# One transformer layer on eight cores: layer-norm output and softmax sums moved from GpSimd to VectorE, value projection done once per stage

## The chip, the cores and the metric

The kernel runs on all 8 cores of one Trainium2 chip. Every core does the same program on its own 4096 of the 32768 tokens, and no core waits for another. The metric is the device time of the slowest core in microseconds (us).

## The reference

The layer attends over the 16 heads of one token, not over tokens, so every token is independent of the others.

```python
q = x @ Wq + bq
kv = (x @ Wdown + bdown) @ Wup + bup
q = q.reshape(B, T, H, Dh)
k, v = jnp.split(kv.reshape(B, T, H, 2 * Dh), 2, axis=-1)
q = apply_rope(q)
k = apply_rope(k)
att = jnp.einsum('bthd,btgd->bthg', q, k) / jnp.sqrt(jnp.float32(Dh))
att = jax.nn.softmax(att, axis=-1)
out = jnp.einsum('bthg,btgd->bthd', att, v)
x = _layernorm(x + out.reshape(B, T, D) @ Wout + bout)
h = jax.nn.silu(x @ wg.T / 127) * (x @ wu.T / 127)
x = _layernorm(x + h @ wdn.T / 127)
```

D is 1024, H is 16, Dh is 64, the latent width is 256 and the hidden width 3072. The rotation of q and k depends on the token alone, and both q and k of a product belong to the same token, so it drops out of att and the kernel leaves it away.

## The kernel before

All activations lie transposed: 128 features in the partitions, tokens along the columns. After a part that turns the weights to bf16 and stores them again in DRAM (the first 350 us), a core works through 8 stages of 512 tokens (`ST`). A stage has a main chain of work, planned into one list per engine:

- `plan_head`: x is loaded by DMAs of the POOL queue (L294), the latent is computed (L313, evacuated by L323), then q with weight tiles `wqb`, eight DMAs of the SP queue into two buffers (matmuls L346, evacuation L357).
- For each half of 256 tokens (`HF`): `plan_kv_part` computes k for all 16 heads (matmuls L588, ScalarE evacuation L603 into `krep`) and then v in the same way into `vdup0` or `vdup1`. `plan_sc` multiplies q by each head's k on VectorE (L622 into `hadb`, two buffers), sums over features on TensorE (L647) and takes the exponential on ScalarE (L634 into `e_sb`).
- `plan_av`: GpSimd adds the 16 exponentials (L668 and fourteen times L674 into `esum32`), VectorE takes the reciprocal (L677), casts it (L679) and scales `e_sb` by it in eight operations (L685). Then, 64 times, TensorE spreads weights to 128 partitions (L738, `selz_sb`), VectorE multiplies them by v (L701 into `p_sb`, two buffers), and TensorE adds up the product (L754, `id_sb`); ScalarE evacuates the sum (L706, `avn`).
- `plan_wo`: output projection with weight tiles `wob` (L792), and the residual on VectorE (L805). The projection of the first half is planned after the scores of the second.
- The first layer norm ends with sixteen VectorE operations of 512 columns, eight times a multiplication (L895) and an addition (L899), which write the input of the feed-forward part.

Beside it, in stage s, runs a second chain, `plan_ffn_ch2`, the feed-forward part of stage s-1: 24 tiles m, each with a gate (L397, eight matmuls) and an up product (L407, eight), `silu` on ScalarE (L416) and a product on VectorE (L423, `h_sb`), then 192 matmuls of the down projection (L450) with their residual (L459). The two weight tiles of an m, `wgb` and `wub`, are DMAs of the POOL queue. Both buffers are double, the second DMA waits until the first has landed since they count on one semaphore, and the gate product waits for both. The second layer norm ends with the scale and shift of the output: for each of 8 pieces GpSimd multiplies (L522 into `lnscr2`) and adds (L530 into `x2b`, two buffers), and a DMA of the SP queue stores the piece to `yt`. The addition of piece J waits until the store of piece J-2 has landed.

The order of the two chains on each engine is set by a list scheduler at build time. It knows a cost `d` of every operation and emits, at each step, the operation that can start first:

```python
key = (round(es / 800.0), -CP[id(nd)], es)
if best is None or key < best[0]:
    best = (key, k, ch, nd, es)
```

Within a chain nothing overtakes on its engine, and at run time each engine goes through its list in order. Changed costs or queues therefore change how the chains are interleaved on all five queues. All DMAs of the second chain and of q and the output projection are written by one helper, L263.

## Time and profile before

| what | value |
|---|---|
| runs shown | 3774.47 and 3853.24 us, median 3813.85 us |
| profiled execution | 3772.72 us, its span 3771.2 us on the slowest core |
| spans of the eight cores | 3746.8 to 3771.2 us |
| mean granted TensorE clock of the slowest core | 0.893 |
| PE busy | 2767.9 us, 73% |
| DVE (VectorE) busy | 1565.3 us, 42% |
| ACT (ScalarE) busy | 823.7 us, 22% |
| POOL (GpSimd) busy | 625.7 us, 17% |

Busy time is the share of the span in which an engine executes; a matmul's busy time holds its latency too, so it overlaps with the next one's. A view of waits names, for each idle gap of an engine, the instruction that ended it. The program starts with 346 us in which TensorE has nothing to do, the stages begin then; stage 0 has no feed-forward part beside it, and after the last stage one feed-forward part runs alone.

### The profile page before, as it was taken

How to read it: one execution, taken by the hardware profiler on the slowest of the kernel's cores; microseconds unless marked ns; L12 is line 12 of the kernel's file. 1: busy time of each engine (PE TensorE's matmuls, PEld its weight loads, DVE VectorE, ACT ScalarE, POOL GpSimd, SP SyncE). 2: the span in 40 equal slices, each digit the busy share in tenths (PEclk: the TensorE clock that was granted, in tenths of full speed). 3: DMA queues.
4: the chain of work that ended last, by engine and by line, in shares of the span. 5: the costliest groups of instructions: out<-in, count | busy, mean ns of one | idle time of the engine just before them, and what ended most of it. 6: DMA issues, size and time to landing. Idle time of an engine off the chain costs nothing.

```text
span 3771.2 us, 42195 instructions; the slowest of 8 cores (3746.8 to 3771.2 us)
## 1 busy us (share of the span) xinstructions
PE 2767.9 (73%) x12672; PEld 1093.4 (29%) x12672; DVE 1565.3 (42%) x2086; ACT 823.7 (22%) x1479; POOL 625.7 (17%) x908
## 2 busy tenths in 40 slices
PE   0002686789877988698968996798779896989565
PEld 0000221333323333233322432333333332333122
DVE  2221444354444444453545353544444445535210
ACT  0000220314023312322140404140233223221100
POOL 0111101011121120312021112111211203110312
PEclk9999665889988999899988999899889998999688
DMA  6886001112231232223221323123312312221222
GB/s 192 241 241 178 9 1 34 51 36 73 78 108 30 65 84 67 73 59 87 71 75 52 92 65 95 40 70 82 94 41 62 89 58 87 62 79 59 95 78 73
DMA packets 108706, 303.98 MB, mean 81 GB/s; under 512 B 16192, under 2 KB 24768, under 8 KB 108496
## 3 DMA queue, kind: packets, MB, share of 16 engines
q1 hardware_dynamic: 61520, 169.14, 15.3%
q0 software_dynamic: 46976, 132.15, 12.2%
q8 instruction: 118, 1.93, 0.2%
q14 instruction: 92, 0.75, 0.1%
HBM read 269.77 MB, written 39.85 MB: 82 GB/s over the span
## 4 chain that ended last, share of the span: by engine, by line
PE 56%; DMA 9%; POOL 8%; issue 7%; DVE 6%; ACT 4%; POOLq 0%; DVEq 0%; ACTq 0%; SPq 0%
PE P L450 10%; PE P L738 9%; PE P L397 8%; PE P L407 8%; PE P L754 7%; PE P L647 6%; POOL esum L674 4%; DMA wgb<-wg_s 3%; DMA wub<-wu_s 3%; PE P L588 3%; DVE p_sb L701 3%; POOL lnscr L522 2%; POOL x2b L530 2%; PE P L792 2%; DVE hadb L622 1%
## 5 line engine op out<-in xcount | busy, mean ns | idle before, releaser
L701 DVE TENSOR_TENSOR p_sb<-P,vdup 128x512 bf16<-128x512 f32 x1024 | 697.7, 690 | 503.9 <-PE P L754 385.5
L397 PE MATMUL P<-x_bf,wgb 128*128 128x512 bf16 x1536 | 535.0, 414 | 163.2 <-DMA wub<-wu_s 163.1
L738 PE MATMUL P<-e_sb,selz_sb 16*128 16x512 bf16 x1024 | 431.5, 430 | 137.7 <-DVE e_sb L685 92.9
L754 PE MATMUL P<-p_sb,id_sb 128*128 128x256 bf16 x2048 | 501.8, 303 | 37.8 <-DVE p_sb L701 33.1
L450 PE MATMUL P<-h_sb,wdb 128*128 128x512 bf16 x1536 | 509.0, 397 | 13.7 <-DVE r_bf L459 13.1
L407 PE MATMUL P<-x_bf,wub 128*128 128x512 bf16 x1536 | 518.8, 399 | 0.0
L622 DVE TENSOR_TENSOR hadb<-q_sb,krep 128x2048 bf16<-128x2048 bf16 x256 | 309.3, 1224 | 431.0 <-PE P L647 292.0
L647 PE MATMUL P<-hadb,selred_sb 128*16 128x256 bf16 x2048 | 325.3, 276 | 45.2 <-DVE hadb L622 19.9
L423 DVE TENSOR_TENSOR h_sb<-s_sil,P 128x512 bf16<-128x512 bf16 x192 | 131.3, 684 | 413.6 <-PE P L407 298.9
L313 PE MATMUL P<-x_bf,wd_sb 128*128 128x512 bf16 x128 | 36.0, 431 | 352.5 <-DMA x_bf<-xt 352.5
L706 ACT ACTIVATE avn<-P 128x256 bf16<-128x256 f32 x128 | 49.2, 384 | 989.7 <-PE P L754 975.6
L397 PEld LDWEIGHTS P<-x_bf,wgb 128*128 128x128 bf16 x1536 | 150.4, 102 | 380.4 <-issue 299.9
L792 PE MATMUL P<-avn,wob 128*128 128x256 bf16 x1024 | 236.5, 283 | 31.0 <-DMA wob<-wout_s 19.4
L263 POOL DMA_DIRECT2D wgb<-wg_s x192 | 105.8, 551 | 896.7 <-PE P L407 818.1
L416 ACT ACTIVATE s_sil<-P 128x512 bf16<-128x512 f32 x192 | 114.4, 596 | 626.1 <-PE P L397 625.6
L754 PEld LDWEIGHTS P<-p_sb,id_sb 128*128 128x128 bf16 x2048 | 180.3, 101 | 229.2 <-issue 187.4
L738 PEld LDWEIGHTS P<-e_sb,selz_sb 16*128 16x128 bf16 x1024 | 91.4, 93 | 485.2 <-issue 485.2
L522 POOL TENSOR_TENSOR lnscr<-r_bf,rstd 128x512 f32<-128x512 bf16 x64 | 84.5, 1321 | 870.1 <-DVE nmb L513 862.1
L647 PEld LDWEIGHTS P<-hadb,selred_sb 128*16 128x16 bf16 x2048 | 153.2, 89 | 216.9 <-issue 193.6
L407 PEld LDWEIGHTS P<-x_bf,wub 128*128 128x128 bf16 x1536 | 153.0, 101 | 209.4 <-issue 112.9
L346 PE MATMUL P<-x_bf,wqb 128*128 128x512 bf16 x512 | 134.4, 415 | 105.8 <-DMA wqb<-wq_s 90.0
L450 PEld LDWEIGHTS P<-h_sb,wdb 128*128 128x128 bf16 x1536 | 146.1, 99 | 218.8 <-issue 124.3
(69 smaller groups left out, 2141.3 us busy)
## 6 DMA issues: line engine op xcount, KB each, us to landing
wdb<-wdn_s SPq DMA_DIRECT2D x64, 768.0 KB, 4.3
wgb<-wg_s POOLq DMA_DIRECT2D x192, 256.0 KB, 3.0
wub<-wu_s POOLq DMA_DIRECT2D x192, 256.0 KB, 2.9
wob<-wout_s SPq DMA_DIRECT2D x128, 256.0 KB, 2.8
wqb<-wq_s SPq DMA_DIRECT2D x64, 256.0 KB, 3.1
yt<-x2b SPq DMA_DIRECT2D x64, 256.0 KB, 2.1
stg<-wg SPq DMA_DIRECT2D x24, 512.0 KB, 5.0
stg<-wu SPq DMA_DIRECT2D x24, 512.0 KB, 5.3
```

The source lines that it names most:

```text
L346: e.matmul(o, l, r, start=st, stop=sp)),
L397: e.matmul(o, l, r, start=st, stop=sp)),
L407: e.matmul(o, l, r, start=st, stop=sp)),
L450: e.matmul(o, l, r, start=st, stop=sp)),
L522: b=rstd2[:, :]: e.tensor_mul(o, a, b)),
L622: add('V', (lambda e, o=o, a=q3, b=b: e.tensor_mul(o, a, b)), waits=tuple(w), inc=s_v, d=1460)
L647: e.matmul(o, l, r, start=st, stop=sp)),
L674: e.tensor_tensor(o, a, b, ALU.add)),
L701: add('V', (lambda e, o=o, a=a, b=b: e.tensor_mul(o, a, b)), waits=w, inc=s_v, d=640)
L738: e.matmul(o, l, r, start=True, stop=True)),
L754: e.matmul(o, id_sb[:, :], r, start=st, stop=sp)),
L792: e.matmul(o, l, r, start=st, stop=sp)),
```

## The change

Three edits. The sixteen operations that scale and shift the output of the second layer norm go from GpSimd to VectorE. The fifteen additions of exponentials go from GpSimd to VectorE, in the main chain. And v is computed once per stage for all 512 tokens into `vdup_all`, by sixteen pairs of 512-column matmuls and sixteen 512-column evacuations, in place of two times sixteen of 256 columns; the multiplication L701 then reads two pieces of 256 columns that lie 512 apart. GpSimd keeps only its DMAs, and its two semaphores are dropped. Line numbers after the change move by some 2 to 24.

```diff
-        vdup = [E(nc.sbuf_tensor(f"vdup{i}", [128, NH * HF], BF16)) for i in range(2)]
+        vdup_all = E(nc.sbuf_tensor("vdup_all", [128, NH * ST], BF16))
...
             for J in range(XC):
-                w = [(s_v2, ck['nmb2_v']), (s_v2, r2_v[J]), (s_gv2, s_gv2.c)]
-                add('G', (lambda e, o=lnscr2[:, :], a=r2_bf[:, J * ST:(J + 1) * ST],
+                add('V', (lambda e, o=lnscr2[:, :], a=r2_bf[:, J * ST:(J + 1) * ST],
                           b=rstd2[:, :]: e.tensor_mul(o, a, b)),
-                    waits=w, inc=s_gv2, d=1000)
-                w = [(s_gv2, s_gv2.c)]
+                    waits=[(s_v2, s_v2.c)], inc=s_v2, d=830)
+                w = [(s_v2, s_v2.c)]
                 val = outb[J % 2] + 16 * (J // 2) if J >= 2 else outb[J % 2]
                 if val > 0:
                     w.append((s_out[J % 2], val))
                 o = x2b[J % 2][:, :]
-                x2_v.append(add('G', (lambda e, o=o, a=lnscr2[:, :], b=nmb2[:, :]:
+                x2_v.append(add('V', (lambda e, o=o, a=lnscr2[:, :], b=nmb2[:, :]:
                                       e.tensor_add(o, a, b)),
-                                waits=w, inc=s_gv2, d=1000))
+                                waits=w, inc=s_v2, d=830))
...
+            def plan_vd():
+                pe0, sc0 = s_pe.c, s_s.c
+                for g in range(NH):
...
+                    for c in range(2):
+                        o = P[5 + g % 2][:, 0:ST]
+                        l = wupv_sb[:, g * 256 + c * 128:g * 256 + (c + 1) * 128]
+                        r = lat_bf[:, c * ST:(c + 1) * ST]
+                        add('T', (lambda e, o=o, l=l, r=r, st=(c == 0), sp=(c == 1):
+                                  e.matmul(o, l, r, start=st, stop=sp)),
...
+                    o = vdup_all[:, g * ST:(g + 1) * ST]
+                    i_ = P[5 + g % 2][:, 0:ST]
+                    b = bupv_sb[:, g:g + 1]
+                    evs.append(add('S', (lambda e, o=o, i=i_, b=b:
+                                         e.activation(o, i, AF.Identity, bias=b)),
+                                   waits=tuple(w), inc=s_s, d=770))
...
                 for g in range(2, NH):
                     a2 = e_sb[:, g * HF:(g + 1) * HF]
-                    add('G', (lambda e, o=esum32[:, :], a=esum32[:, :], b=a2:
+                    add('V', (lambda e, o=esum32[:, :], a=esum32[:, :], b=a2:
                               e.tensor_tensor(o, a, b, ALU.add)),
-                        waits=[(s_s, exp_g(g)), (s_gv, s_gv.c)], inc=s_gv, d=450)
+                        waits=[(s_s, exp_g(g)), (s_v, s_v.c)], inc=s_v, d=420)
...
-                        b = vdup[hf][:, gp * 512:(gp + 1) * 512]
+                        b = vdup_all[0:128, 0:NH * ST].rearrange(
+                            "p (g t) -> p g t", g=NH)[:, 2 * gp:2 * gp + 2,
+                                                      hf * HF:hf * HF + HF]
...
             kd0 = plan_kv_part(0, 0)
-            vd0 = plan_kv_part(0, 1)
+            vd_all = plan_vd()
             exp_end0, had0 = plan_sc(0, kd0)
-            avn_end0, erep_end0 = plan_av(0, exp_end0, vd0)
+            avn_end0, erep_end0 = plan_av(0, exp_end0, vd_all)
             kd1 = plan_kv_part(1, 0, guard=[(s_v, ck['avtt_end'][0])])
-            vd1 = plan_kv_part(1, 1)
```

The scheduler's new order shows in three places.

First, SyncE's queue (SP) at a boundary of two stages. Before, with `wqb` the weight tiles of q for the next stage, `yt` the stores of the finished output and `wdb` tiles of the down projection:

```order
L263 DMA wqb<-wq_s 128x1024 x2
L263 DMA yt<-x2b 128x512 x3
L263 DMA wqb<-wq_s 128x1024
L263 DMA yt<-x2b 128x512
L263 DMA wqb<-wq_s 128x1024
L263 DMA yt<-x2b 128x512
L263 DMA wqb<-wq_s 128x1024
L263 DMA yt<-x2b 128x512
L263 DMA wqb<-wq_s 128x1024
L263 DMA yt<-x2b 128x512 x2
L263 DMA wdb<-wdn_s 128x3072 x2
L263 DMA wqb<-wq_s 128x1024 x2
```

and now:

```order
L261 DMA wqb<-wq_s 128x1024 x2
L261 DMA yt<-x2b 128x512 x2
L261 DMA wqb<-wq_s 128x1024 x6
L261 DMA yt<-x2b 128x512
L261 DMA wob<-wout_s 128x1024
L261 DMA yt<-x2b 128x512
L261 DMA wob<-wout_s 128x1024
L261 DMA yt<-x2b 128x512 x4
L261 DMA wdb<-wdn_s 128x3072 x2
```

The stores of the output stood between the tiles of q; now all tiles of q but the first two stand together, and six stores and the two down tiles stand behind them. In the other boundaries seven tiles stand ahead of the first store.

Second, GpSimd's queue (POOL) from the same boundary into the next stage. Before:

```order
L522 TENSOR_TENSOR lnscr<-r_bf,rstd 128x512
L530 TENSOR_TENSOR x2b<-lnscr,nmb 128x512
L263 DMA wgb<-wg_s 128x1024
L263 DMA wub<-wu_s 128x1024
L263 DMA wgb<-wg_s 128x1024
L263 DMA wub<-wu_s 128x1024
L668 TENSOR_TENSOR esum<-e_sb 16x256
L674 TENSOR_TENSOR esum<-esum,e_sb 16x256 x14
L263 DMA wgb<-wg_s 128x1024
L263 DMA wub<-wu_s 128x1024
```

and now:

```order
L292 DMA x_bf<-xt 128x512 x8
L261 DMA wgb<-wg_s 128x1024
L261 DMA wub<-wu_s 128x1024
L261 DMA wgb<-wg_s 128x1024
L261 DMA wub<-wu_s 128x1024
L261 DMA wgb<-wg_s 128x1024
L261 DMA wub<-wu_s 128x1024
```

The weights of the first two tiles stood behind the output of the layer norm, and those of the third behind the additions of exponentials; both are gone from the queue.

Third, TensorE at the end of the scores of a first half (`hadb`) and the begin of the weighted sum (`selz_sb`). Before:

```order
L647 MATMUL P<-hadb,selred_sb 16x256 x24
L407 MATMUL P<-x_bf,wub 128x512
L397 MATMUL P<-x_bf,wgb 128x512 x8
L407 MATMUL P<-x_bf,wub 128x512 x8
L738 MATMUL P<-e_sb,selz_sb 128x512 x2
L397 MATMUL P<-x_bf,wgb 128x512 x4
L738 MATMUL P<-e_sb,selz_sb 128x512
```

and now, from the last of the scores on (ahead of it stand the up product of m=0, the 16 matmuls of m=1, and the last two groups of scores with five gate matmuls of m=2 between them):

```order
L671 MATMUL P<-hadb,selred_sb 16x256
L395 MATMUL P<-x_bf,wgb 128x512 x3
L405 MATMUL P<-x_bf,wub 128x512 x8
L395 MATMUL P<-x_bf,wgb 128x512 x8
L762 MATMUL P<-e_sb,selz_sb 128x512 x2
L405 MATMUL P<-x_bf,wub 128x512 x8
L762 MATMUL P<-e_sb,selz_sb 128x512
```

Some 24 more matmuls of the feed-forward part (m=2 whole, the gate of m=3) now stand ahead of the weighted sum. Of the second half's k part, where 56 feed-forward matmuls stood between 64 of k and v, 30 now stand between 32 of k.

## Rows read from the trace of the kernel before

**Rows 1.** Windows (us; busy PE, PEld, DVE, ACT, POOL; clock; DMA; GB/s): a stage, a part
```profile
1901.00:2298.60 397.60, 331.00 (x1586) 134.06 (x1584) 187.05 (x248) 105.40 (x188) 68.28 (x100) 0.94 0.24 71
...
2074.70:2096.10 21.40, 20.40 (x121) 10.54 (x120) 4.45 (x6) 16.74 (x37) 3.42 (x7) 1.00 0.26 76
```

**Rows 2.** Waits of PE over the whole span: us in total, times, longest
```profile
PE P L397 <- DMA wub<-wu_s: 163.1, 58, 26.8
PE P L738 <- DVE e_sb L685: 92.9, 10, 15.6
PE P L346 <- DMA wqb<-wq_s: 90.0, 33, 13.5
```

**Rows 3.** Timeline of a boundary: start, us, engine, operation [idle before it <-what ended it]
```profile
1903.04 1.57 DVE L895 TENSOR_TENSOR lnscr<-r_bf,rstd 128x512 f32<-128x512 bf16 x1
...
1904.20 1.43 POOL L522 TENSOR_TENSOR lnscr<-r_bf,rstd 128x512 f32<-128x512 bf16 x1
...
1920.18 0.61 POOL L263 DMA_DIRECT2D wgb<-wg_s  x1
...
1920.80 0.82 SPq L263 DMA_DIRECT2D wdb<-wdn_s  x2
...
1927.90 0.55 POOL L263 DMA_DIRECT2D wub<-wu_s  x1 [7.11 <-DMA wgb<-wg_s]
...
1932.62 5.16 PE L346 MATMUL P<-x_bf,wqb 128*128 128x512 bf16 x16 [13.48 <-DMA wqb<-wq_s]
```

**Rows 4.** Timeline of PE in the q part after stage 0
```profile
710.42 3.61 PE L346 MATMUL P<-x_bf,wqb 128*128 128x512 bf16 x16 [0.93 <-ACT lat_bf L323]
...
725.02 3.80 PE L346 MATMUL P<-x_bf,wqb 128*128 128x512 bf16 x16 [0.77 <-DMA wqb<-wq_s]
```

**Rows 5.** ACT: evacuations of v in one half (timeline), of k and q (groups, mean ns)
```profile
1947.39 8.68 ACT L603 ACTIVATE vdup<-P,bupv_sb 128x256 bf16<-128x256 f32 x16
...
L603 ACT ACTIVATE krep<-P,bupk_sb 128x256 bf16<-128x256 f32 x256 | 118.5, 474 | 56.5 <-PE P L588 55.0 <-issue 0.3
...
L357 ACT ACTIVATE q_sb<-P,bq_sb 128x512 bf16<-128x512 f32 x64 | 44.0, 687 | 194.0 <-PE P L346 194.0
```

**Rows 6.** Timeline from the additions of exponentials to the first weighted sums
```profile
1977.67 11.09 POOL L674 TENSOR_TENSOR esum<-esum,e_sb 16x256 f32<-16x256 f32 x14
...
1988.93 1.74 DVE L677 RECIPROCAL zinv<-esum 16x256 f32<-16x256 f32 x1 [6.10 <-POOL esum L674]
...
1990.77 0.28 DVE L679 CAST zinvb<-zinv 16x256 bf16<-16x256 f32 x1
...
1991.72 1.10 PE L738 MATMUL P<-e_sb,selz_sb 16*128 16x512 bf16 x2 [10.00 <-DVE e_sb L685]
...
1995.31 1.87 PE L397 MATMUL P<-x_bf,wgb 128*128 128x512 bf16 x4 [2.49 <-DMA wub<-wu_s]
```

**Rows 7.** VectorE's prices: groups by line, mean ns after the busy time
```profile
L701 DVE TENSOR_TENSOR p_sb<-P,vdup 128x512 bf16<-128x512 f32 x1024 | 697.7, 690 | 503.9 <-PE P L754 385.5 <-PE P L738 116.1 <-issue 0.3
...
L622 DVE TENSOR_TENSOR hadb<-q_sb,krep 128x2048 bf16<-128x2048 bf16 x256 | 309.3, 1224 | 431.0 <-PE P L647 292.0 <-PE P L588 76.1 <-ACT krep L603 57.6
...
L501 DVE TENSOR_TENSOR vpe<-vpe,musq 128x512 f32<-128x512 f32 x8 | 5.5, 692 | 29.1 <-ACT musq L498 29.1
```

**Rows 8.** Timeline: two weight DMAs of POOL in the first half's output projection
```profile
2150.98 0.55 POOL L263 DMA_DIRECT2D wgb<-wg_s  x1 [2.18 <-PE P L407]
...
2157.44 0.55 POOL L263 DMA_DIRECT2D wgb<-wg_s  x1 [1.99 <-PE P L407]
```

**Rows 9.** Timeline of DVE before the last feed-forward part, of POOL at the end
```profile
3521.22 0.69 DVE L899 TENSOR_TENSOR x_bf<-lnscr,nmb 128x512 bf16<-128x512 f32 x1
3530.73 0.69 DVE L423 TENSOR_TENSOR h_sb<-s_sil,P 128x512 bf16<-128x512 bf16 x1 [8.82 <-PE P L407]
...
3740.23 1.15 POOL L522 TENSOR_TENSOR lnscr<-r_bf,rstd 128x512 f32<-128x512 bf16 x1 [70.82 <-DVE nmb L513]
...
3760.95 1.26 POOL L530 TENSOR_TENSOR x2b<-lnscr,nmb 128x512 f32<-128x512 f32 x1 [0.20 <-POOL lnscr L522]
```

More of the change, by code:

```diff
@@ L574, in plan_kv_part @@
                 pe0, sc0 = s_pe.c, s_s.c
-                wgt = wupk_sb if part == 0 else wupv_sb
+                wgt = wupk_sb
                 for g in range(NH):
@@ L591, in plan_kv_part @@
                 for g in range(NH):
-                    dst = krep if part == 0 else vdup[hf]
-                    bias = bupk_sb if part == 0 else bupv_sb
+                    dst = krep
+                    bias = bupk_sb
                     w = list(wS([(s_pe, pe0 + g + 1)]))
                     if g == 0:
-                        if part == 0 and prev_red_end:
+                        if prev_red_end:
                             w.append((s_pe, prev_red_end))
-                        if part == 1 and ck['avtt_end'][hf]:
-                            w.append((s_v, ck['avtt_end'][hf]))
                     o, i_ = dst[:, g * HF:(g + 1) * HF], P[5 + g % 2][:, 0:HF]
@@ L604, in plan_kv_part @@
                                    waits=tuple(w), inc=s_s, d=560))
+                return evs
+            def plan_vd():
+                pe0, sc0 = s_pe.c, s_s.c
+                for g in range(NH):
+                    w = []
+                    if sc0 + g - 1 > 0:
+                        w.append((s_s, sc0 + g - 1))
+                    for c in range(2):
[4 more added lines that the diff above has]
+                                  e.matmul(o, l, r, start=st, stop=sp)),
+                            waits=(w if c == 0 else ()),
+                            inc=(s_pe if c == 1 else None), d=258)
+                evs = []
+                for g in range(NH):
+                    w = list(wS([(s_pe, pe0 + g + 1)]))
+                    if g == 0:
+                        for h2 in range(2):
+                            if ck['avtt_end'][h2]:
+                                w.append((s_v, ck['avtt_end'][h2]))
+                    o = vdup_all[:, g * ST:(g + 1) * ST]
[4 more added lines that the diff above has]
+                                   waits=tuple(w), inc=s_s, d=770))
                 return evs
@@ L666, in plan_av @@
                 exp_g = lambda g: exp_end - NH + g + 1
[L667 removed]
+                add('V', (lambda e, o=esum32[:, :], a=e_sb[:, 0:HF],
                           b=e_sb[:, HF:2 * HF]: e.tensor_tensor(o, a, b, ALU.add)),
[L669 to L670 removed]
+                    waits=wV([(s_s, exp_g(1)), (s_v, s_v.c)]), inc=s_v, d=420)
                 for g in range(2, NH):
                     a2 = e_sb[:, g * HF:(g + 1) * HF]
[L673 removed]
+                    add('V', (lambda e, o=esum32[:, :], a=esum32[:, :], b=a2:
                               e.tensor_tensor(o, a, b, ALU.add)),
[L675 to L676 removed]
+                        waits=[(s_s, exp_g(g)), (s_v, s_v.c)], inc=s_v, d=420)
                 add('V', (lambda e, o=zinv[:, :], i=esum32[:, :]: e.reciprocal(o, i)),
[L678 removed]
+                    waits=[(s_v, s_v.c)], inc=s_v, d=2100)
                 add('V', (lambda e, o=zinvb[:, :], i=zinv[:, :]: e.tensor_copy(o, i)),
```

23 lines of the change are left out of this document (8 added, 15 removed).

## The prediction, made before the changed kernel ran

> **What bounds the kernel now.** I read the page first, then the busy time of one stage, the waits of PE, and last the timeline of that stage queue by queue. A stage takes 397.6 us, of which PE is busy 331 us and DVE 187 us [rows 1]. PE does everything else waits for, so what counts is where PE stands still. Leaving the start aside, its three largest waits are 163.1 us for the weights of the feed-forward part, 92.9 us for the normalized exponentials and 90.0 us for the weights of q [rows 2]. All three lead to GpSimd. At a boundary of two stages GpSimd scales the output with operations of 1.43 us; each store to `yt` waits for one, and SyncE's queue holds the weights of q between and behind these stores, so that the last two q tiles come after 13.48 us of standing still [rows 3]. The next feed-forward weights are issued behind the same GpSimd work, at 1920.18, and the first of them needs until 1927.90 [rows 3]. Inside the stage GpSimd adds exponentials for 12 us while PE waits 10.0 us, and the weights of the third tile stand behind these additions, for another 2.49 us [rows 6]. Nothing of this is GpSimd being busy, which it is for 68 of 397.6 us; it is GpSimd's queue.
>
> **The q part (-72 us).** After stage 0 there is no second layer norm, hence no store and no GpSimd work. There the q part shows what the q tiles cost by themselves: 16 matmuls in 3.6 us, then gaps of about 0.8 us, three in all [rows 4]. Eight q parts with 2.3 us of such gaps are 18 us; the rest of the 90.0 us [rows 2], 72 us, comes from the stores, and the new order has at least six of the eight tiles in a row. What takes its place: DVE does both layer norms alone. Now they run side by side and hinder each other, 1.57 us for an operation that takes 0.69 us alone [rows 3, 9]. Sixteen of DVE's operations beside GpSimd's take about 1.6 us each with the gap, 26 us; on DVE alone 32 operations of 0.69 us and 0.1 us between them are 25 us. So the pair of norms is done as early as before, the output simply comes last. An addition that waits for a store holds up what is queued behind it on DVE, the multiplications of q by k (L622). The first two of those are ready when the q part ends, and PE needs them only after k and v, over 20 us later (8.7 us for each, [rows 5]). I count nothing for it.
>
> **v at once (+24 us), and its second half gone (-71 us).** An evacuation of 256 columns takes 0.474 us and comes every 0.54 us (8.68 by 16), because PE and ACT take turns on two banks. With 512 columns ACT needs 0.687 us, 0.21 more, and PE 0.22 more (3.61 us for 16 matmuls of 512 columns, so two times 256 columns more) [rows 4, 5]. Two banks share this, so one comes every 0.54 + 0.21 = 0.75 us: 12.1 us in place of 8.7 us in the first half, +3.4 us in 7 stages. In the second half PE's list had 56 feed-forward matmuls of 512 columns and 64 of 256 columns in the k and v part of 21.4 us [rows 1]; it now has 30 and 32. By columns that is 52%, 11.2 us, so 10.2 us less in 7 stages. The weights say the same: a tile pair comes every 6.46 us there [rows 8], and 26 matmuls are 1.6 pairs, 10.5 us. Those 26 are done earlier, in the 10 us in which PE stood still.
>
> **Sums of exponentials, first half (-29 us).** DVE's price for 16x256 float32 additions stands in no row. From below it is the cast of the same size, 0.28 us, from above GpSimd's own 0.79 us (11.09 by 14) [rows 6]. Between them I take 0.42 us: a 512-column addition takes 0.692 us and L622, which does its 2048 columns at two per step, 1.224 us for 1024 steps [rows 7], so a step costs 1.04 ns and an operation 0.16 us beside them. With 0.10 us between two operations (1988.93 + 1.74 to 1990.77) 15 of them take 7.8 us against 12.0 us: 4.2 us. The Trainium skill, page "VectorE: DVE Perf Modes", section on the TRN2 errata, gives (N+151)/0.96 ns for a float32 addition of two tensors of N columns, which it calls exact at 512, 691 ns; the trace agrees at 512 (692 ns). No run here shows 256 columns; by the page it would be 424 ns. Off the 4.2 us go two products of the feed-forward part (L423, 0.69 us) that now stand between on DVE, 1.4 us, and eight up matmuls ahead of the third broadcast on PE, some 1.1 us of which nothing hides. To it come the 2.49 us of waiting for weights [rows 6]. That makes 4.2 us in 7 stages. The new order asks for four weight tiles in a row between the up product of m=0 and the first weighted sum: at 3.2 us each (half of 6.46, [rows 8]) they have landed some 11 us after it and the gate of m=3 is done at 13.7 us; DVE's chain, counted from the same point (1.0 us for a group of scores, 1.2 us for the last multiplication, additions, reciprocal 1.74 us, cast, first scaling), ends at about 14 us. So DVE still is the last, by little.
>
> **Second half and the rest (-14, -14, -19 us).** In the second half the additions are on the path too, 4.2 us less 1.4 us of products between them; PE's list holds feed-forward work up to there, so I take 2 us in 7 stages. Stage 0 has no feed-forward part: twice 4.2 us, and v falls from 17.4 to 12.1 us, 13.7 us together. At the end, the last feed-forward part starts with weights already loaded: its first product came at 3530.73, 8.8 us after the layer norm had ended [rows 9]. With both norms on DVE the input is ready some 6 us earlier too, at about 3516, and one gate and up product at half clock takes about 4 us more; I take 10 us. The last output is 22 us of GpSimd work (3740.23 to 3762.21) [rows 9], on DVE 12.8 us, stretched to 13.5 us by the landing of stores: -8.5 us.
>
> Sum: -72 +24 -71 -29 -14 -14 -19 = -195 us. From the profiled execution's 3773 us this gives 3578 us, 5.2% less. The profiled execution lies with the lower of the two runs shown (3774); the median, 3814, holds one of 3853, and such a run of the changed kernel would be at 3650.
>
> **Rivals.** *The weights take the place of the additions.* The four tiles ahead of the weighted sum may come slowly: next to stores and `wdb` one took 7.7 us (1920.18 to 1927.90, [rows 3]) in place of 3.2. Four of them cost 18 us; less 3 us of slack and again in 7 stages that is +105 us: 3683 us. For it speaks that stores now trail into the next stage; against it that the scores come 40 us after the boundary, and that tiles in the middle of a stage come every 3.2 us [rows 8].
>
> *The moved work is worth nothing.* DVE becomes the late one: stores that wait in SyncE's queue hold its additions, q by k comes late, and the 72 us are lost; an addition costs GpSimd's 0.79 us, and 16 times 4.2 us are lost. 3578 + 72 + 67 = 3717 us, 1.5% under before. Against it: DVE is busy 187 of 397.6 us [rows 1] and gets 8 us a half and 13 us a boundary. The Trainium skill, page "Perfetto Trace Analysis", section on optimizing Scalar and DVE operations, says work may go to GpSimd when DVE is saturated, and that a move between the two might not help since they share a read port. The trace shows the sharing, 1.57 against 0.69 us, and by it the pair of norms alone gives nothing; what I expect comes from the two queues behind it.
>
> *Slower: v read with a stride.* L701 runs 1024 times, on the path, and now reads two pieces. At 0.69 us [rows 7] with 0.53 us of it for the 512 columns (1.04 ns each), half speed would give 3578 + 543 = 4121 us. It decides from 0.19 us each, and 0.27 us each are 2% slower. Against it: L622 reads q in eight pieces and k repeated, and does 2048 columns in 1224 ns [rows 7], twice the rate of L501.
>
> **How the numbers follow.** The forecast 0.65, the weights 0.17, worth nothing 0.10, the stride 0.04, something unnamed 0.04. By its own unknowns the forecast reaches down to 3500 us: additions at 0.38 us a piece are 34 us less, v hidden 24 us less, the boundaries a little shorter than counted, 20 us. Upwards, additions at 0.79 us add 67 us, and most of the rival on weights lies under 3680 us. Hence 3500 to 3680 us. Faster by over 2%, which is about what a measurement of this kernel can tell, holds the forecast, the weights and a little of the rest: 0.85; within 2% 0.10, slower 0.05.
>
> **What would show it.** Right: PE's wait for `wqb` falls from 90 to about 20 us; the additions on DVE at 0.42 us, reciprocals 8 us after the last multiplication by k; evacuations of v every 0.75 us; the k part of the second half near 11 us; L701 still at 690 ns; a stage some 23 us shorter. Wrong: waits for `wub` ahead of L738 in each stage, a wait of `x2b` for a store that reaches PE, or L701 above 0.7 us.

## The result, and the profile after

The changed kernel takes 3525.72 us (median of 11 runs, 3509.68 to 3711.7) beside 3773.32 us of the kernel before (10 runs); the ratio is 0.934, 95% interval 0.9311 to 0.9369, so 6.6% faster. The profiled execution took 3518.16 us, its span 3516.3 us, against 3771.2 us before. The forecast was 3578 us, range 3500 to 3680. Ratios below are always to the kernel before, with their 95% interval. Where half of the chip ran at a lower clock in a profiled execution (runs 5 and 8), its numbers here are those of a core of the other half.

Lines move by 2 to 24: L344 is the q part, L395 and L405 gate and up product, L585 k, L613 and L627 v, L646 the multiplication of q by k, L671 the scores, L692 and L697 the additions, L725, L762 and L778 the weighted sums, L816 the projection, L918 and L922 the first layer norm, L519 and L527 the output.

First the windows of a whole stage and of the k part of a second half, which answer to [rows 1]:

```profile
core 7: us, PE busy (x) PEld busy (x) DVE busy (x) ACT busy (x) POOL busy (x), PEclk, DMA share, GB/s
1790.50:2155.60 365.10, 326.22 (x1553) 130.79 (x1552) 197.52 (x291) 102.49 (x171) 30.55 (x56) 0.97 0.26 78
1947.90:1959.30 11.40, 10.81 (x64) 5.36 (x62) 3.28 (x4) 8.29 (x19) 1.78 (x4) 1.00 0.26 74
```

The stage is 32.5 us shorter while PE's busy time fell only from 331 to 326 us: the gain is time in which PE stood still. VectorE took over all the arithmetic of GpSimd and is busy only 10 us more. The column behind POOL says that the granted clock rose too, from 0.94 to 0.97. The waits of PE over the whole span answer to [rows 2]:

```profile
PE P L395 <- DMA wub<-wu_s: 93.0, 52, 6.6
PE P L344 <- DMA wqb<-wq_s: 40.0, 30, 2.9
PE P L762 <- DVE e_sb L707: 20.6, 2, 11.2
PE P L395 <- DVE x2b L527: 19.3, 1, 19.3
```

The three waits of [rows 2] came to 346 us and are 154 us now. The fourth line has a new name only: at the same place, ahead of the first gate product of the last feed-forward part, PE stood still before as well, and longer, and the view put it down to the weights, which were loaded behind GpSimd's output work. It is the longest wait in the first line of [rows 2]:

```profile
3524.31 3.57 PE L397 MATMUL P<-x_bf,wgb 128*128 128x512 bf16 x8 [26.80 <-DMA wub<-wu_s]
```

So of the 70 us by which the wait for `wub` fell, 26.8 us changed their name, and 19.3 us of them are still there. The boundary of two stages, as [rows 3] showed it (DVE, PE and SyncE's queue):

```profile
1795.58 0.69 DVE L918 TENSOR_TENSOR lnscr<-r_bf,rstd 128x512 f32<-128x512 bf16 x1
...
1797.87 12.13 SPq L261 DMA_DIRECT2D wqb<-wq_s  x6
1810.15 0.34 SPq L261 DMA_DIRECT2D yt<-x2b  x1
...
1811.52 3.65 PE L344 MATMUL P<-x_bf,wqb 128*128 128x512 bf16 x16 [1.93 <-DMA wqb<-wq_s]
```

Six q tiles are issued in a row and PE's gaps between them are at most 1.93 us, where one was 13.48 us. The groups by line answer to [rows 5] and [rows 7], the timeline behind the scores to [rows 6]:

```profile
L725 DVE TENSOR_TENSOR p_sb<-P,vdup_all 128x512 bf16<-128x512 f32 x1024 | 697.5, 689 | 448.2 <-PE P L778 312.5 <-PE P L762 133.5
...
L697 DVE TENSOR_TENSOR esum<-esum,e_sb 16x256 f32<-16x256 f32 x224 | 92.3, 412 | 25.2 <-ACT e_sb L658 3.6 <-DVE esum L697 0.5
...
L918 DVE TENSOR_TENSOR lnscr<-r_bf,rstd 128x512 f32<-128x512 bf16 x64 | 44.2, 691 | 6.2
...
L527 DVE TENSOR_TENSOR x2b<-lnscr,nmb 128x512 f32<-128x512 f32 x64 | 44.2, 691 | 30.1 <-DMA yt<-x2b 22.8 <-DVE lnscr L519 7.1
```
```profile
1824.88 12.05 ACT L627 ACTIVATE vdup_all<-P,bupv_sb 128x512 bf16<-128x512 f32 x16
...
1858.89 6.10 DVE L697 TENSOR_TENSOR esum<-esum,e_sb 16x256 f32<-16x256 f32 x12
...
1865.69 0.47 ACT L658 ACTIVATE e_sb<-P,cvec_sb 16x256 bf16<-16x256 f32 x1 [2.38 <-PE P L671]
...
1866.33 0.41 DVE L697 TENSOR_TENSOR esum<-esum,e_sb 16x256 f32<-16x256 f32 x1 [0.40 <-ACT e_sb L658]
```

An addition costs 412 ns (0.42 us forecast), L725 with its stride 689 ns (690 before), a layer-norm operation 691 ns (1309 beside GpSimd), an evacuation of v comes every 0.75 us (12.05 by 16, as forecast). The last three lines show something the forecast did not have: twelve additions are done before the last exponential exists; the chain of additions waits for it, not the other way round. The last exponential is late because the added feed-forward matmuls stand among the last scores.

The timelines of PE show where the time went. Each line is the length of one part of PE's list, from its first matmul to its last or to the next part, in us and summed over the seven stages 1 to 7; the last three lines are single stretches:

| part of PE's list | before | after | change |
|---|---|---|---|
| q parts | 209.7 | 145.3 | -64.4 |
| k of the first half | 84.9 | 66.3 | -18.6 |
| v of the first half | 60.8 | 85.7 | +24.9 |
| first score to first weighted sum | 251.2 | 233.4 | -17.8 |
| weighted sums, first half | 582.5 | 541.9 | -40.6 |
| k (and v) of the second half | 152.0 | 78.7 | -73.3 |
| projection to second weighted sum | 297.9 | 283.8 | -14.1 |
| weighted sums, second half | 581.9 | 550.3 | -31.6 |
| second projection | 159.7 | 170.4 | +10.7 |
| stage 0 | 358.5 | 341.1 | -17.4 |
| after the last projection | 282.8 | 273.8 | -9.0 |
| start of stage 0 | 346 | 344 | -2 |

With the small parts left out (-2) this is the 255 us between the spans. Two changes stand out, for the forecast had no term for them: the weighted sums of both halves, 72 us, whose own matmuls are as before, and the k part of the first half.

### The profile page after: what moved, and what is told of

Same layout as the page of the kernel before. It is cut to its first block, busy times and chain, and to the rows that moved or that the text cites. A ratio compares the mean times of both kernels' runs of the same rounds, so it can differ in the third digit from the quotient of the medians.

```text
span 3516.3 us, 41208 instructions; the slowest of 8 cores (3489.0 to 3516.3 us)
## 1 busy us (share of the span) xinstructions
PE 2687.4 (76%) x12416; PEld 1059.3 (30%) x12416; DVE 1668.7 (47%) x2454; ACT 807.4 (23%) x1363; POOL 292.2 (8%) x540
## 3 DMA queue, kind: packets, MB, share of 16 engines
q1 hardware_dynamic: 61520, 169.14, 16.5%
## 4 chain that ended last, share of the span: by engine, by line
PE 60%; DMA 11%; DVE 8%; issue 6%; ACT 5%; DVEq 0%; ACTq 0%; POOLq 0%; POOL 0%; SPq 0%
PE P L448 10%; PE P L762 9%; PE P L395 9%; PE P L405 8%; PE P L778 8%; PE P L671 6%; DMA wgb<-wg_s 3%; DMA wub<-wu_s 3%; DVE p_sb L725 3%; PE P L816 2%; PE P L344 2%; DMA wqb<-wq_s 2%; PE P L585 2%; PE P L613 2%; DMA wob<-wout_s 1%
## 5 line engine op out<-in xcount | busy, mean ns | idle before, releaser
L725 DVE TENSOR_TENSOR p_sb<-P,vdup_all 128x512 bf16<-128x512 f32 x1024 | 697.5, 689 | 448.2 <-PE P L778 312.5
L395 PE MATMUL P<-x_bf,wgb 128*128 128x512 bf16 x1536 | 524.2, 402 | 113.6 <-DMA wub<-wu_s 93.0
L405 PE MATMUL P<-x_bf,wub 128*128 128x512 bf16 x1536 | 494.0, 395 | 22.8 <-DVE h_sb L421 22.8
L778 PE MATMUL P<-p_sb,id_sb 128*128 128x256 bf16 x2048 | 487.0, 292 | 26.7 <-DVE p_sb L725 19.9
L448 PE MATMUL P<-h_sb,wdb 128*128 128x512 bf16 x1536 | 495.1, 387 | 13.3 <-DVE r_bf L457 12.3
L646 DVE TENSOR_TENSOR hadb<-q_sb,krep 128x2048 bf16<-128x2048 bf16 x256 | 309.6, 1223 | 349.2 <-PE P L671 261.8
L762 PE MATMUL P<-e_sb,selz_sb 16*128 16x512 bf16 x1024 | 414.3, 413 | 65.5 <-DVE p_sb L725 43.2
L671 PE MATMUL P<-hadb,selred_sb 128*16 128x256 bf16 x2048 | 327.6, 275 | 44.3 <-DVE hadb L646 19.0
L816 PE MATMUL P<-avn,wob 128*128 128x256 bf16 x1024 | 243.4, 285 | 40.0 <-DMA wob<-wout_s 28.8
L395 PEld LDWEIGHTS P<-x_bf,wgb 128*128 128x128 bf16 x1536 | 149.0, 100 | 340.3 <-issue 242.7
L778 PEld LDWEIGHTS P<-p_sb,id_sb 128*128 128x128 bf16 x2048 | 176.2, 99 | 210.1 <-issue 163.1
L671 PEld LDWEIGHTS P<-hadb,selred_sb 128*16 128x16 bf16 x2048 | 152.2, 88 | 219.5 <-issue 198.0
L405 PEld LDWEIGHTS P<-x_bf,wub 128*128 128x128 bf16 x1536 | 150.0, 100 | 225.1 <-issue 122.8
L762 PEld LDWEIGHTS P<-e_sb,selz_sb 16*128 16x128 bf16 x1024 | 90.6, 92 | 392.5 <-issue 392.5
L829 DVE SCALAR_TENSOR_TENSOR r_bf<-P,bout_sb,x_bf 128x256 bf16<-128x256 f32 x128 | 61.7, 482 | 258.2 <-PE P L816 258.2
L658 ACT ACTIVATE e_sb<-P,cvec_sb 16x256 bf16<-16x256 f32 x256 | 117.5, 465 | 228.6 <-PE P L671 228.0
```

What stands on the lines that cost most here:

```text
L395: e.matmul(o, l, r, start=st, stop=sp)),
L405: e.matmul(o, l, r, start=st, stop=sp)),
L448: e.matmul(o, l, r, start=st, stop=sp)),
L646: add('V', (lambda e, o=o, a=q3, b=b: e.tensor_mul(o, a, b)), waits=tuple(w), inc=s_v, d=1460)
L658: e.activation(o, i, AF.Exp, bias=b, scale=0.125)),
L671: e.matmul(o, l, r, start=st, stop=sp)),
```

## The experiments

Theory Q: the first edit acts through the two queues in which GpSimd's operations and the stores stood. Theory C: the weighted sums are shorter because PE no longer stands still ahead of them, and with that no longer falls to half clock (1.2 in place of 2.4 GHz, a granted clock of 0.50). The rivals: E (the first edit makes VectorE faster), O (the weighted sums are shorter through another order of the matmuls), and in the expectations of runs 6 and 7 O' (the half clock in them comes from the boundary of the stages).

**1. First edit undone.** The sixteen operations of L519 and L527 go back to `'G'` with a semaphore of their own, as in the removed lines of the diff.

> The changed kernel with the sixteen output operations of the second layer norm back on GpSimd, all else as changed. Theory Q (what the move brought is order in two queues): the stores stand between the q tiles on SyncE again, the q parts go from 126 back to about 185 us in seven stages, PE's wait for wqb from 40 to about 100 us, the first k part waits again for feed-forward weights in some stages (+20 us), the last output takes 9 us longer: about 3526 + 92 = 3618 us. Rival E (what it brought is a faster VectorE, or the q part was shortened by the other two edits): the q parts stay under 145 us, and the time rises by no more than 30 us, to 3556 us or less.

Ratio to before 0.958 (0.9523 to 0.9637), in the profile's run 3617 us. The q parts are at 204.1 us in seven stages (145.3 with the edit; the table below has all such sums), the first k parts at 86.2 (66.3), and what follows the last projection takes 288.3 us (273.8):

```profile
PE P L396 <- DMA wub<-wu_s: 134.1, 51, 27.5
PE P L345 <- DMA wqb<-wq_s: 87.6, 34, 11.1
```

As Q said. Rival E is out by the time; the next run tests it again with both engines loaded as here.

**2. The same, but GpSimd issues the stores.**

```diff
-            for J in range(XC):
                 w = [(s_gv2, x2_v[J])]
...
-                dma('Y', s_out[J % 2], dst, src, w)
+                dma('G', s_out[J % 2], dst, src, w)
```

> As the first run, but GpSimd issues the stores of the output itself, so SyncE's queue holds the eight q tiles in a row while GpSimd and VectorE still work side by side. Theory Q: the q parts stay at 120 to 135 us, so about 60 us less than the first run, 3558 us, unless the weights of the feed-forward part, now behind operations and stores on GpSimd, take it back in part. Rival E (sharing between the two engines is what costs): no better than the first run, q parts near 185 us, 3618 us.

The q parts are 152.4 us and PE waits as little for `wqb` as in the changed kernel, while GpSimd and VectorE still work side by side. That settles the q part: it was SyncE's order. But the time is 3718 us, ratio 0.9848 (0.98 to 0.9895). That is worse than the first run, and 160 us above the 3558 us expected:

```profile
PE P L396 <- DMA wub<-wu_s: 168.3, 45, 15.9
PE P L817 <- DMA wob<-wout_s: 73.3, 40, 8.7
...
PE P L345 <- DMA wqb<-wq_s: 35.8, 28, 3.7
```
```profile
1852.22 0.58 POOL L262 DMA_DIRECT2D yt<-x2b  x1 [0.59 <-POOL x2b L529]
...
1856.25 0.58 POOL L262 DMA_DIRECT2D yt<-x2b  x1 [0.56 <-POOL x2b L529]
...
1877.04 0.58 POOL L262 DMA_DIRECT2D yt<-x2b  x1 [0.56 <-POOL x2b L529]
1877.62 0.55 POOL L262 DMA_DIRECT2D wgb<-wg_s  x1
1881.46 0.55 POOL L262 DMA_DIRECT2D wub<-wu_s  x1 [3.29 <-DMA wgb<-wg_s]
```

Each store now costs GpSimd's queue 4 us with its two operations, and the feed-forward weights stand behind all eight: the first k parts grow to 141.2 us. The second projection grows too (211.0 us), since in the new order of SyncE's queue two tiles of the down projection stand ahead of the last two of `wob`; run 11 shows this again. In both kernels the queue that holds the stores between its loads takes the stall.

**3. Second edit undone.** The additions go back to `'G'`.

> The changed kernel with the fifteen additions back on GpSimd. Both theories: PE's wait for e_sb goes from 20.6 back to about 90 us, from the end of scores to the weighted sum 2 to 4 us more in each of 16 halves, some 35 to 60 us. Theory C (the weighted sums became shorter, 83 to 78 us, because PE no longer stands still ahead of them and keeps its clock): the granted clock in the weighted sums falls from 0.98 to 1.00 back to about 0.92 and each of the first halves takes about 83 us: +40 us more or +72 us with the second halves, so 3600 to 3650 us. Rival O (they became shorter through another interleaving of feed-forward matmuls, which v at once brought): weighted sums stay at 77 to 79 us, 3560 to 3585 us.

Ratio 0.9516 (0.9482 to 0.9551), the profiled run 3598 us. The first weighted sums take 535.1 us in seven stages, even less than 541.9: Theory C in the form in which I had put it fails here, and of the two expectations O's holds for the weighted sums; the time, 3590 us by the ratio, lies between the two ranges. PE's wait for `e_sb` is 29.4 us, where both had about 90; what grows is the wait for `wub`, 165.2 us against 93.0. The reason is in the timeline: the order, too, is another than before, the piece of 10.00 us [rows 6] is 5.68 us here and ends with the weights, whose DMAs stand between and behind the additions in GpSimd's queue, and the half clock that follows it lies over a gate product that stands ahead of the first weighted sum, where it makes "score to weighted sum" longer (285.5 us) instead:

```profile
1908.18 3.57 PE L396 MATMUL P<-x_bf,wgb 128*128 128x512 bf16 x8 [5.68 <-DMA wub<-wu_s]
1911.68 0.60 PE L765 MATMUL P<-e_sb,selz_sb 16*128 16x512 bf16 x1
```

Eight gate matmuls take 3.57 us there, 1.89 us at full clock. The unit must be the sum of both: 820.6 us here, 775.3 us with the edit.

**4. Third edit undone.** v in two parts of 256 tokens.

> The changed kernel with v in two halves of 256 tokens again. Its own terms: k and v of the second half 21.4 in place of 10.7 us in eight stages, v of the first 8.7 in place of 12.2: +10.2 x 7 + 8.7 - 3.5 x 8, about +50 us, 3576 us. Theory C: nothing else, the weighted sums stay at 77 to 79 us with clocks of 0.98 to 1.00. Rival O: the weighted sums go back to 83 us in 14 halves, +70 us more, 3646 us.

Ratio 0.951 (0.9458 to 0.9562). k and v of the second half take 152.4 us and v of the first 63.7: the edit's own terms are as forecast. The weighted sums take 551.5 and 549.1 us, 79 us each: not rival O's 83 us, so v at once isn't what shortened them here. Some 64 us were lost where 50 were expected.

**5. The waiting alone.** VectorE is held up, and the order of all lists stays: by tiles, the traces show every engine's list as in the changed kernel, but for the reciprocals put in:

```diff
+                for _ in range(NX):
+                    add('V', (lambda e, o=zinv[:, :], i=esum32[:, :]: e.reciprocal(o, i)),
+                        waits=[(s_v, s_v.c)], inc=s_v, d=0)
```

NX is 6 in first halves and 0 in second ones.

> The changed kernel with six more reciprocals of the same sums (a result already there) in each first half, between the sums and the scaling, planned at cost 0 so that every list keeps its order. They hold VectorE 6 x 1.74 us, so PE stands still some 10 us more ahead of the first weighted sum, as it did before the change; their own cost is 8 x 10.5 = 84 us less what feed-forward work catches up, which PE can't do since the order is fixed. Theory C (a stand-still of 10 us brings a stretch at half clock that outlasts it): granted clock at 0.50 for 10 to 15 us after work resumes, first weighted sums 83 us in place of 77.4, so +40 us: 3526 + 84 + 40 = 3650 us. Rival O (their length came from the order): first weighted sums stay at 77 to 79 us, 3610 us.

Ratio 0.9627 (0.9553 to 0.97), about 3633 us. The profile has 308.7 us from first score to weighted sum (233.4), the 75 us that the reciprocals cost, and first weighted sums of 566.6 us: 24.7 us more with the same instructions in the same order. Rival O, by which nothing should have changed, can't explain these. Two stages, each in windows of the last feed-forward work, the waiting, the first 17 us of weighted sums, the rest; the column behind POOL is the granted clock:

```profile
1150.00:1163.90 13.90, 12.16 (x59) 4.91 (x58) 11.81 (x21) 6.43 (x8) 2.74 (x5) 1.00 0.26 75
1163.90:1174.80 10.90, 0.04 (x1) 0.07 (x1) 10.07 (x9) 0.60 (x1) 0.55 (x1) 0.61 0.16 48
1174.80:1192.00 17.20, 15.63 (x41) 4.57 (x42) 9.28 (x17) 0.60 (x1) 1.09 (x2) 0.50 0.11 32
1192.00:1258.00 66.00, 62.00 (x284) 23.46 (x289) 42.63 (x64) 6.86 (x14) 8.11 (x15) 0.99 0.20 57
...
1547.50:1558.40 10.90, 0.02 (x1) 0.02 (x1) 10.08 (x9) 0.60 (x1) 0.55 (x1) 0.70 0.17 48
1558.40:1575.00 16.60, 14.34 (x53) 4.67 (x54) 10.64 (x20) 0.98 (x2) 1.09 (x2) 0.78 0.12 33
```

So C's mechanism exists: a stand-still brings the engine to 1.2 GHz, and it stays there while it is busy again: 41 matmuls in 17.2 us where 53 are done in 16.6. But of one and the same stand-still of 10.9 us one is followed by 17 us at half clock and the other by some 7. Three of seven first weighted sums took 83 us, four 79 us. Of the +40 us expected 25 came.

**6 and 10. First edit alone**, on the kernel before. Both runs are of the same kernel.

> The kernel before with the first edit alone (output of the second layer norm on VectorE). Theory Q: q parts at 19 to 24 us and no wait for feed-forward weights in the first k part, so 99 us less than before, as much as its undoing cost: 3674 us. Theory C: the 10 us of waiting for the additions ahead of the first weighted sum are still there in one piece, so its weighted sums stay at 82 to 86 us at a clock of 0.84 to 0.92. Rival O' (the half clock in the weighted sums came from the boundary, by some carry-over): weighted sums fall to 77 to 79 us with this edit alone, some 70 us more gained, 3605 us.

> The sixth run's kernel once more, for a profile whose clock is not disturbed. Theory C: granted clock 0.84 to 0.95 and 82 to 86 us in the first weighted sums, since 10 us of waiting stand ahead of each. Rival O': 77 to 79 us at 0.98 or more.

Ratio 0.9752 (0.9665 to 0.9839) in the sixth run; the tenth run's profile (3682 us, 3674 expected) has q parts of 139.2 us, first k parts of 66.9 and first weighted sums of 598.5 us, 83 to 93 us each. Repairing the boundary does nothing for them, against O'. Windows of stage 3's waiting and the first 16.5 us of its weighted sums:

```profile
1541.50:1554.50 13.00, 3.72 (x18) 1.46 (x15) 3.81 (x5) 1.88 (x2) 8.90 (x14) 0.84 0.07 21
1554.50:1571.00 16.50, 13.71 (x35) 3.79 (x36) 7.84 (x15) 0.60 (x1) 1.63 (x3) 0.50 0.15 48
```

**7. Second edit alone.**

> The kernel before with the second edit alone (additions on VectorE). Theory C: what PE waits ahead of the first weighted sum falls from 10 to about 5 us, and the first weighted sums to 77 to 79 us; with additions and weights (+52 +25 in the third run) and the shorter weighted sums the gain is 90 to 140 us, 3635 to 3685 us. Rival O': weighted sums still at 83 us, gain 50 to 80 us, 3695 to 3725 us.

Ratio 0.9736 (0.9664 to 0.9808), some 100 us gained, as C had it (90 to 140). The first weighted sums fall from 582.5 to 560.5 us, 80 us each where C had 77 to 79 and O' 83, the second from 581.9 to 553.9, the way from first score to weighted sum from 251.2 to 219.2 us. The prediction's terms for this edit, stage 0 included, came to 51 us.

**9. Third edit alone.**

> The kernel before with the third edit alone (v once per stage). Its own terms are the 50 us of the fourth run's forecast: 3724 us. Theory C: the piece of 10 us ahead of the first weighted sum is as it was, and the weighted sums stay at 82 to 86 us; nothing beyond the 50 us. Rival: what the fourth run lost beyond its own terms (64 us for 50) belongs to this edit, then 3705 us or less.

Ratio 0.9783 (0.9737 to 0.9829), 82 us gained for 50 expected, and weighted sums of 535.2 us with the additions still on GpSimd: my expectation of C was wrong, for the reason of run 3. In the sum of scores, or projection, and weighted sums this edit gains 10 us in first halves and 15 us in second ones. With that every combination of the edits is measured (us, seven stages; "first half" and "second half" run from the first score, or the projection, to the end of the weighted sums):

| edits made | q parts | first k | first half | second half | k(+v) 2nd | after last projection | ratio |
|---|---|---|---|---|---|---|---|
| none | 209.7 | 84.9 | 833.7 | 879.8 | 152.0 | 282.8 | 1 |
| output | 139.2 | 66.9 | 847.7 | 885.1 | 152.0 | 270.0 | 0.975 |
| sums | 190.3 | 89.0 | 779.7 | 844.9 | 152.3 | 284.5 | 0.974 |
| v | 209.5 | 82.4 | 823.2 | 864.7 | 77.5 | 291.0 | 0.978 |
| output, sums | 147.7 | 65.3 | 779.2 | 832.0 | 152.4 | 273.8 | 0.951 |
| output, v | 140.3 | 66.7 | 820.6 | 867.0 | 78.0 | 271.6 | 0.952 |
| sums, v | 204.1 | 86.2 | 779.5 | 835.1 | 78.6 | 288.3 | 0.958 |
| all | 145.3 | 66.3 | 775.3 | 834.1 | 78.7 | 273.8 | 0.934 |

Each column follows one edit in the main: the q parts and first k parts the output, the two halves the sums, the k part v. In first halves the sums are worth 44 to 68 us, in second ones 30 to 53 us, whatever else is done.

The traces of these eight kernels also answer what the weighted sums follow. Of their 56 first weighted sums in stages 1 to 7, the 17 with under 1.5 us at half clock take 75 to 78 us, the 11 with 13 to 19 us of it 81 to 84 us, and the five with over 20 us 84 to 93 us; the others take 77 to 83 us. This holds whatever edits the kernel has and whatever order they brought. For the order itself that leaves at most some 3 us apiece; what else it does is to decide whether a stretch at half clock falls into the weighted sums or beside them.

**8. The wait that is left.** The DMA of an up tile waits until the gate tile has landed, for both count on one semaphore.

```diff
-                dma('G', s_gd[m % 2], d2, r2s)
+                dma('G', s_gu[m % 2], d2, r2s, w)
```

(and the products wait for the one or the other).

> The changed kernel with a semaphore of its own for each up tile, so that the DMA of an up tile no longer waits until the gate tile has landed. PE's largest wait that is left is for these (93.0 us, 52 times). If the wait is the two DMAs in a row (3.2 us each), it falls below 30 us and the time by 40 to 65 us: 3460 to 3485 us. Rival (they wait for DMA engines, which are busy with each other's transfers): 3.2 us each becomes 5 to 6 us side by side, and less than 15 us are gained.

The best of its four runs took 3460 us, too few to give a ratio; the four cores read in the profiled one took 3459 to 3476 us. So some 40 to 60 us are gained, and the rival of the busy DMA engines is out. But all of it is the last feed-forward part, 208.5 us in place of 273.8. Windows of that part, after (219 us) and here (155 us):

```profile
3281.00:3500.00 219.00, 156.35 (x573) 61.49 (x571) 22.18 (x34) 22.91 (x37) 23.83 (x44) 0.82 0.24 75
```
```profile
3305.00:3460.00 155.00, 132.20 (x580) 55.00 (x578) 23.44 (x34) 23.19 (x38) 24.09 (x44) 0.96 0.34 108
```

Of the 93.0 us of waiting for `wub` 47.9 lay there, and the same matmuls also lost their full clock. In the stages the other 45 us of waits went away and the stages got no shorter (2574 us for seven, 2557 in the changed kernel): weighted sums took 16 and 11 us more. A wait removed there seems only to move feed-forward work, until something else is in the way; no run isolates what.

**11. First gate and the output's place**, on the eighth run's kernel.

```diff
-            ck['ffn'] = dict(x1_v=x1_v, pe2_prev=s_pe2.c, v2_prev=s_v2.c,
+            ck['ffn'] = dict(x1_v=x1_v, pe2_prev=s_pe2.c, v2_prev=ck['nmb2_v'],
```

and the output operations and their stores are a chain of their own for the scheduler. The first gate product then no longer waits for the output's last piece.

> The eighth run's kernel, and the first gate product no longer waits for the last output piece of the stage before (its semaphore count is taken at the second layer norm's last statistic), with the first layer norm going ahead of the output. The tail of the eighth run was 208.5 us, of which 19.7 us were PE waiting for x2b. If that wait is only the layer norms' own time on VectorE, 3 to 5 us are gained and the first product of the last part follows the last output projection by some 33 us in place of 38; if the count was the cause, 10 us or more. The time: 3470 us, in any case the fastest yet.

VectorE's first product of the last part (`h_sb`) comes 32.4 us after the last projection (37.9 in the changed kernel, 38.8 in the eighth run), and what follows that projection takes 199.9 us: 6 us gained ahead of that product, a little over the 3 to 5 expected. So the wait of 19.3 us is for the most part the two layer norms' own work, and the count on VectorE's semaphore, on which the output now runs too, at most 6 us of it. The best run took 3481 us (3470 expected), ratio 0.9215 (0.9179 to 0.9251), no better than the eighth run. The second projections take 222.8 us in place of 176. SyncE's queue there, and PE:

```profile
2135.94 9.76 SPq L263 DMA_DIRECT2D wob<-wout_s  x4
2148.83 0.85 SPq L263 DMA_DIRECT2D wdb<-wdn_s  x2
2151.16 2.38 SPq L263 DMA_DIRECT2D wob<-wout_s  x2
```
```profile
2159.53 0.37 PE L821 MATMUL P<-avn,wob 128*128 128x256 bf16 x1 [6.01 <-DMA wob<-wout_s]
```

Two tiles of the next down projection, of 768 KB each, got ahead of the last two tiles of the projection; these were issued from 2151.16 on and PE had the last at 2159.53, in 8 us where such a tile takes 3.0 in the changed kernel. In the changed kernel the two stand behind the stores. What one edit gives at the end, the order takes in each stage: PE's wait for `wob` is 74.3 us (28.8 in the changed kernel).

**12. Additions among the scores**, on the eleventh run's kernel.

```diff
                     add('V', (lambda e, o=o, a=q3, b=b: e.tensor_mul(o, a, b)),
                         waits=tuple(w), inc=s_v, d=1460)
+                    had_v.append(s_v.c)
+                    if g >= 3:
+                        esum_add(g - 2, sc0)
```

> The eleventh run's kernel with each addition of an exponential placed two multiplications of q by k behind its score, not after all sixteen. In the first halves VectorE does both at 1.31 us a head and gains nothing, or loses 0.5 us a head from the scores, given back behind them: no change. In the second halves the additions leave the path behind the residuals of the first half's projection, 7.5 us less between projection and weighted sum in 8 halves: -50 us, 3420 us. Rival (PE is full there with feed-forward work, which only moves elsewhere): within 15 us of the eleventh run.

Ratio 0.9115 (0.9071 to 0.9159), the profiled run 3446 us: the fastest kernel of this study, 2.4% under the changed one (0.9115 by 0.934). The second half between projection and weighted sum, VectorE's timeline:

```profile
2025.28 0.48 DVE L839 SCALAR_TENSOR_TENSOR r_bf<-P,bout_sb,x_bf 128x256 bf16<-128x256 f32 x1 [0.40 <-PE P L826]
2025.87 1.74 DVE L709 RECIPROCAL zinv<-esum 16x256 f32<-16x256 f32 x1
```

In the changed kernel the additions stood there for 8 us (2028.55 to 2036.6). From projection to weighted sum it is 200.0 us in seven stages against 258.0 in the eleventh run, but the stages shorten by only 37 us: the scores of the second half take 15 us more and the first weighted sums 567 in place of 531 us, with half clock again in four of seven. As expected in place and sign, but the time lies some 20 us above the 3420 us expected.

## Why the prediction was right, term by term

The terms were on the right waits and of the right sign, and the two on v fit within 3 us. That the time lies in the range is partly luck: its lower part was kept for cheaper additions (0.38 us), a hidden v and shorter boundaries, none of which came, and two gains that no term had, 91 us together, filled it.

**q part, -72 forecast, -64 measured.** The mechanism is shown by runs 1 and 2: SyncE's order, not VectorE's speed. But the term was worked out as waits alone, and they fell from 90.0 to 40.0 us, not to the 20 us named as a sign. The rest goes with the clock, which had no term: the q parts of stages 1 to 7 held some 61 us at half clock before and hold 7 us now, and the 16 matmuls behind the wait of 13.48 us [rows 3] took 5.16 us where the last 16 of that part now take 3.65 us. The gaps came out at 5.0 us a part (40.0 by 8) where stage 1 had given 2.3. Most boundaries still have one store ahead of the last tile, but the gaps are 4.5 us also where six tiles follow each other, so what makes a tile later than in stage 1 is open. The additions that wait for stores (22.8 us in all) didn't reach PE through the multiplications of q by k: its waits for `hadb` are 19.0 us, 19.9 before.

**The weights behind GpSimd, missing.** The step "What bounds the kernel now" named the next feed-forward weights issued at 1920.18 behind GpSimd's work, and then no term counted them. The first k part stalled on them in three stages; the part is 18.6 us shorter now. It takes 82 to 89 us in every kernel of the table with the output on GpSimd and 65 to 67 us in every one without.

**v, +24 and -71 forecast, +24.9 and -73.3 measured.** The best terms: both prices came from rows of the operations themselves.

**Sums, first half -29 and second half -14 forecast.** Here a size was off, by a factor of 1.7 to 2.8: the sums are worth 73 to 122 us in 14 halves by the table. The price of an addition was right. The direct gain in first halves, from first score to weighted sum, was -32.0 us with this edit alone, as forecast, but only -17.8 us in the changed kernel, where the feed-forward matmuls among the last scores delay the last exponential. What the term lacked is what PE's stand-still does to the clock afterwards. The windows of the kernel before, of the waiting in [rows 6] and of the next 16.3 us, would have told:

```profile
1981.70:1991.70 10.00, 0.02 (x1) 0.01 (x1) 3.15 (x5) 0.27 (x1) 6.43 (x10) 0.76 0.09 27
1991.70:2008.00 16.30, 13.79 (x37) 3.94 (x38) 7.89 (x15) 0.60 (x1) 1.64 (x3) 0.52 0.15 48
2008.00:2075.00 67.00, 63.15 (x291) 23.02 (x289) 43.37 (x65) 7.06 (x15) 8.22 (x15) 1.00 0.21 60
```

Summed over slices of 3 us (length by twice the share of the clock that is missing) the weighted sums of both halves held 209 us at half clock before and hold 42 us now: 167 us less, and the sums are 72 us shorter, 0.43 us for each. The kernels with the output edit alone and with the sums alone have 243 and 79 us. Run 5 shows that waiting alone brings such stretches. That the 72 us are time at half clock is borne out by the eight kernels above, where weighted sums free of it take the same 75 to 78 us in any order; how much of the half clock the shorter waits took away, and how much the new order, isn't shown, for with the sums' edit the order changes too. Ahead of second weighted sums PE waited for the weights behind the additions in GpSimd's queue, the gate matmuls behind that wait took twice their time, and after the change the wait is down to 2.08 us, though these matmuls still take 3.26 us; before and after:

```profile
2173.06 3.57 PE L397 MATMUL P<-x_bf,wgb 128*128 128x512 bf16 x8 [4.84 <-DMA wub<-wu_s]
```
```profile
2036.26 3.26 PE L395 MATMUL P<-x_bf,wgb 128*128 128x512 bf16 x8 [2.08 <-DMA wub<-wu_s]
```

**Stage 0, -14 forecast, -17.4 measured. The end, -19 forecast, -9 measured.** The last output fell as forecast, from 22 to 13.2 us, with no wait for a store. The start of the last part, taken at VectorE's first product as in the prediction, did not come 10 us earlier but 4.5 (37.9 us after the projection, 42.4 before): the weights are now loaded in time, but on VectorE the two layer norms take turns, and the input is complete at 3276.2, 33.7 us after the projection, as before (3521.9, 33.5 us). The step "the input is ready some 6 us earlier" was wrong. The other waits for `wub` in this part grew by 5 us, from 42.9 to 47.9 us. Kernels of the table that differ in this edit alone differ by 11 to 19 us at this end.

In all 195 us forecast and 255 found; the misses were waits and clock that stood in the profile of the kernel before and had no price. The rivals: the weights took nobody's place (their wait fell from 163.1 to 93.0 us, or from 136.3 without the one that changed its name), the moved work was not worth nothing (the first two edits together give 4.9%, each of the three alone 2.2 to 2.6%, with intervals that end between 1.6 and 1.9%), the stride costs nothing (689 ns). The Trainium skill, page "VectorE: DVE Perf Modes", section on the TRN2 errata, would give 424 ns for 256 columns, an estimate by its formula. The trace has 412 ns, so the formula, exact at 512 here (691 ns), is 3% high at 256. The sentence of the Trainium skill, page "Perfetto Trace Analysis", section on optimizing Scalar and DVE operations, that a move between VectorE and GpSimd might not help fits the pair of norms here (33.7 and 33.5 us) and not the kernel, because of what waits in the queues.

## What to carry to other kernels

A slow engine that also issues DMAs, or whose results are stored by a queue that also loads weights, can cost more by what stands behind it in those queues than by its busy time; list the queue's next entries before pricing it, and when such work is moved, look at where every store lands (run 2 lost 100 us against run 1 by the place of the stores, and run 11 lost 47 us against run 8 in the second projections by that of two weight tiles). Price a stand-still of TensorE with the granted clock of the stretch behind it, not only with its own length. When a scheduler reorders, compare sums over neighbouring parts, since a stall moves from one into the next.

## What was not expected of the hardware

The same stand-still of 10.9 us was followed by about 17 us or about 7 us at 1.2 GHz with the same instructions (run 5), and a stretch at half clock also came in the middle of dense work, with no gap over 0.73 us in the 27 us ahead. Three windows of the changed kernel's weighted sums show it:

```profile
1306.00:1325.00 19.00, 17.37 (x81) 6.17 (x79) 11.78 (x18) 1.40 (x3) 1.20 (x3) 1.00 0.29 92
1325.00:1337.00 12.00, 11.99 (x37) 4.02 (x37) 4.84 (x8) 0.63 (x1) 0.00 (x0) 0.57 0.13 52
1337.00:1384.00 47.00, 45.36 (x205) 16.34 (x203) 29.45 (x44) 1.92 (x5) 0.00 (x0) 1.00 0.20 61
```

What brings the engine down there is open; nothing was tried that isolates it. Also left open: a kernel with run 12's additions and run 8's order of SyncE's queue, which by the sums above might be the fastest, was not run.
